# Two-layer gated feed-forward kernel on one core: W_dec in one transfer, gathers in four steps, t's low part on VectorE, new issue orders

## The reference, cut to what matters

```python
# layer 0: a weight matrix of its own for each of 128 sequences, then 8 experts, the best 2 of each token
U = (cond_512 @ W_dec + b_dec).reshape(B, 129, 30)
param = einsum('bik,kj->bij', U, V)
c = einsum('bsd,bde->bse', x, param[:, :-1]) + param[:, -1][:, None]
gate = c @ Wg.T + bg;  w = softmax(top_k(gate, 2))
x = x + sum over the two of w * (W2[e] @ gelu(W1[e] @ c + b1[e]) + b2[e])
# layer 1: layer norms of x with gathered gains and biases, an MLP with a layer norm, then a feed-forward
h = ln(ln(x, pw[id125]), cp[id5]); t = ln(x, tm[id5]); s = ln(x, ms[id3])
m, n, r = x + mlp_ln(memory), x + mlp_ln(noise), x + mlp_ln(resource)
y = ln(silu(concat(w0 h, w1 t, w2 m, w3 n, w4 r, w5 s) @ int_W1 + b1) @ int_W2 + b2, g, be)
f = silu(s1 * (y @ w1)) * (s2 * (y @ w2))
x = x + s5 * (gelu(s4 * (gelu(s3 * (f @ h1)) @ h2)) @ w3)
```

## Time and profile before

| | us |
|---|---|
| median of 3 runs | 443.49 |
| lowest, highest | 441.01, 443.49 |
| the profiled run | 443.04 |
| its span, first to last instruction | 441.2 |
| TensorE busy | 416.0 |
| VectorE busy | 315.6 |
| ScalarE busy | 290.7 |
| GpSimd busy | 142.8 |
| mean granted clock of TensorE | 0.978 |

### The profile page before, as it was taken

The page is one execution under the profiler, slowest core; times in us unless marked ns, Lnnn a source line. Parts: engine busy times, 40 slices in busy tenths (PEclk is TensorE's granted clock), DMA queues, the critical chain, the costliest instruction groups (busy, mean ns, idle before and its releaser), DMA issues.

```text
span 441.2 us, 5719 instructions
## 1 busy us (share of the span) xinstructions
PE 416.0 (94%) x1804; PEld 272.6 (62%) x1804; DVE 315.6 (72%) x651; ACT 290.7 (66%) x515; POOL 142.8 (32%) x129
## 2 busy tenths in 40 slices
...
GB/s 242 364 293 161 179 174 119 112 229 68 104 155 51 71 163 97 118 99 73 111 40 159 75 116 150 0 70 181 134 3 49 46 3 0 1 0 25 0 25 27
DMA packets 29961, 45.08 MB, mean 102 GB/s; under 512 B 3461, under 2 KB 22378, under 8 KB 29418
## 3 DMA queue, kind: packets, MB, share of 16 engines
...
...
## 4 chain that ended last, share of the span: by engine, by line
PE 79%; DVE 8%; ACT 5%; issue 3%; DMA 2%; POOL 2%; another core or an unknown queue 1%; ACTq 0%; POOLq 0%; DVEq 0%
PE bank L644 23%; PE bank L746 20%; PE bank L692 7%; PE bank L636 6%; PE bank L782 6%; PE bank L731 5%; PE bank L823 2%; PE bank L660 2%; DMA muT<-cond_512T_in 2%; PE bank L699 2%; PE bank L771 2%; POOL rstd L1446 1%; ACT mG L890 1%; ACT YN L895 1%
## 5 line engine op out<-in xcount | busy, mean ns | idle before, releaser
L644 PE MATMUL bank<-mG,W 128*128 128x512 f32 x256 | 121.3, 604 | 0.1
L890 ACT ACTIVATE mG<-bank,keepP 128x512 f32<-128x512 f32 x128 | 85.3, 685 | 32.2 <-PE bank L636 30.2
L1446 POOL TENSOR_TENSOR rstd<-ve,mhalf 128x4 f32<-128x4 f32 x24 | 34.0, 1419 | 173.0 <-DVE ve L1196 172.1
L1181 DVE TENSOR_TENSOR mG<-mG,gwbs 128x1024 f32<-128x1024 f32 x64 | 77.1, 1220 | 8.8 <-ACT mG L890 4.4
L644 PEld LDWEIGHTS bank<-mG,W 128*128 128x128 f32 x256 | 48.4, 194 | 44.2 <-issue 39.9
L636 PE MATMUL bank<-ts,A 96*128 96x512 f32 x128 | 66.8, 553 | 1.3 <-ACT mG L890 1.1
L955 ACT ACTIVATE G<-bank,keepP 128x512 f32<-128x512 f32 x48 | 32.8, 696 | 25.4 <-PE bank L746 20.1
L1427 POOL DMA_INDIRECT gp<-pgb_in,ixall x32 | 36.8, 1149 | 27.4 <-DVE norms L1233 17.7
L1430 POOL DMA_INDIRECT gcm<-ctm,ixcm x32 | 36.5, 1140 | 9.8 <-issue 9.8
L746 PE MATMUL bank<-hA_h,h1w_h 128*128 128x512 f32 x96 | 38.9, 405 | 0.0
L746 PE MATMUL bank<-hA_l,h1w_h 128*128 128x512 f32 x96 | 38.6, 402 | 0.0
...
## 6 DMA issues: line engine op xcount, KB each, us to landing
...
```

Of the source, the lines that this page charges most:

```text
L644: mm = pe.matmul(OACC[:, :], W2[:, e * HC + c, :], mG[n % NMG][:, c, :], start=False, stop=(e == E - 1 and c == HC - 1))
L890: act.activation(mG[e % NMG][:, c % HC, :], HM[n % 2][:, :], ACT.Gelu, bias=b1c[:, c:c + 1]).then_inc(m_gelu, 1)
L1181: dve.tensor_tensor(mine, mine, gate.unsqueeze(1).broadcast_to([P, HC, TT, P]), ALU.mult).then_inc(m_q, 1)
L1446: step(pool.tensor_tensor(rstd[:, n, :], ve[:, n, :], mhalf[:, :], ALU.pow))
```

## The change

W_dec comes in one transfer of 128 rows on SP's queue (the halves change their partitions), its last 30 columns (`wd_u`) in one of their own. On ScalarE's queue muT comes first, then `wd_u`, the biases, V, `keepP`, `earlyP`. Piece 7 of the turned W_dec goes to ScalarE. `sq_`, `hs1` and `cs12` move behind G8. The gathers `tab` are issued in four steps of two (`tab0` to `tab3`), each a word of its own in GpSimd's order. `tcl` of blocks 3 to 7 is an instruction of VectorE; blocks 0 to 2 stay on GpSimd. In block 7's feed-forward the copies and low parts of the last two chunks (k of 10 and 11) are single. The order in which the weights are split is h2, h1, w3, w12 instead of h1, h2, w12, w3. All orders are new.

```diff
-        PIECES = ("v", "v", "v", "a", "v", "a", "v", "v")
+        PIECES = ("v", "v", "v", "a", "v", "a", "v", "a")
...
+        def alone(j, k):
+
+            return j is TAIL["p"] and k >= 3 * FC - 2
+
         def tail_lo(eng, j, k):
 
-            eng.wait_ge(p_lo[j.s], j.n * (FC + 4) + (k + 1 if k < FC else FC + (k - FC) // 2 + 1))
+            eng.wait_ge(p_lo[j.s], k + 1 if k < FC else FC + (k - FC) // 2 + 1 + (alone(j, k) and k % 2))
...
             "PE": (
-                (0, "tm0 A0 gm0 A1 sq0 A2 tm1 tm2 gx0 A3 tm3 sq1 tm4 H0 gm1 gm2 H1 H2 tm5 H3 H4 tm6 H5 gm3 sq2 H6 B H7 O0 H8 O1 H9 "
-                    "sq3 H10 H11 O2 H12 H13 O3 H14 gx1 tm7 H15 O4"),
-                (1, "H0 -O5 -O6 H1 H2 -O7 H3 gm4 gm5 H4 -XT H5 H6 B H7 O0 H8 O1 H9 O2 H10 H11 O3 H12 -Tt H13 gm6 H14 H15 gm7 O4"),
...
-                (7, "H0 -O5 H1 =Ts ~F1 H2 -O6 H3 -O7 =Th ~F2 =Z -XT H4 H5 ~F3 B O0 H6 O1 H7 H8 ~F4 H9 ~F5 ~F6 ~F7 =Y O2 H10 -Tt ~F8 "
-                    "-Ts ~F9 -Th ~F10 H11 =YT ~F11 H12 H13 -Z ~F12 =F0 H14 O3 -Y =F1 O4 O5 H15 =F2 O6 O7 =F3 XT -YT -Fr0 =F4 =F5 Tt "
-                    "=F6 Ts =F7 Th -Fr1 Z -Fr2 =F8 Y -Fr3 =F9 =F10 =F11 YT -Fr4 -Fr5 Fp0 -Fr6 -Fr7 =F12 Fp1 -Fr8 Fp2 -Fr9 Fp3 -Fr10 "
-                    "-Fr11 Fp4 Fp5 Fp6 Fp7 -Fr12 Fp8 Fp9 Fp10 Fp11 Fp12"),
+                (0, "tm0 A0 tm1 gm0 sq0 A1 A2 tm2 tm3 gx0 sq1 A3 tm4 tm5 gm1 gm2 H0 H1 H2 H3 H4 sq2 B H5 H6 O0 H7 gm3 H8 O1 H9 H10 "
+                    "O2 H11 H12 sq3 H13 H14 O3 H15 gx1 O4"),
+                (1, "H0 H1 -O5 gm4 H2 -O6 H3 tm6 H4 -O7 H5 tm7 H6 H7 -XT H8 B O0 gm5 H9 O1 H10 H11 O2 H12 O3 H13 O4 H14 H15 gm6 O5"),
...
+                (7, "H0 -O5 H1 ~F1 =Ts H2 -O6 H3 H4 ~F2 =Th -O7 H5 H6 ~F3 =Z -XT B ~F4 H7 ~F5 ~F6 ~F7 H8 H9 -Tt =Y O0 -Ts O1 ~F8 "
+                    "~F9 ~F10 H10 -Th =YT H11 ~F11 H12 -Z ~F12 =F0 -Y O2 =F1 H13 O3 H14 H15 =F2 O4 O5 -YT =F3 O6 O7 XT -Fr0 =F4 =F5 "
+                    "-Fr1 =F6 =F7 Tt -Fr2 Ts =F8 =F9 Th -Fr3 Z =F10 Y =F11 -Fr4 -Fr5 YT -Fr6 -Fr7 Fp0 =F12 Fp1 -Fr8 Fp2 -Fr9 Fp3 "
+                    "-Fr10 -Fr11 Fp4 Fp5 Fp6 Fp7 -Fr12 Fp8 Fp9 Fp10 Fp11 Fp12"),
...
             "ACT": (
-                (0, "gh ah0 aw gel ah1 tch0 gth0 tcg0 ah2 sza gxc0 gxh0 tch1 tcg1 ah3 tch2 tcg2 bh ws g0 g1 tch3 g2 tcg3 g3 smh0 "
-                    "tch4 g4 g5 g6 g7 syc g8 g9 wh1 gth1 g10 g11 wh0 g12 g13 smh1 gxh1 gxc1 g14 g15 tch5 smh2 wh2"),
...
-                    "-nh -tc ~fg8 -sc =ny g9 ~fg9 ~fh8 g10 g11 =ff -ch ~fg10 =fhi ~fg11 ~fh10 g12 -zt =th0 g13 =fh0 =th1 g14 -ny "
-                    "g15 =th2 =fh1 =fh2 =th3 -ff -fhi =fh3 nx -thr0 =fg4 =fg5 =fh4 tc nh sc -fhr0 ch =fg6 -thr1 =fg7 =fh6 -fhr1 zt "
...
+                (0, "aw ah0 gh tch0 tch1 tcg0 tcg1 gel gth0 ah1 bh sza ah2 gxh0 gxc0 tch2 ws ah3 tcg2 wh1 tch3 g0 g1 g2 g3 g4 syc "
+                    "g5 tcg3 g6 wh2 tch4 g7 tcg4 g8 g9 g10 tch5 smh0 wh0 gth1 g11 g12 g13 g14 gxh1 gxc1 g15 smh1"),
...
+                    "=fh1 =th2 -ny g15 =fh2 =th3 -ff -fhi =fh3 -thr0 nx -thr1 =fg4 =fg5 =fh4 =fg6 =fg7 =fh6 tc -fhr0 -thr2 nh sc "
+                    "-fhr1 ch -fhr2 -thr3 zt -fhr3 =fg8 =fg9 =fg10 =fg11 =fh8 ny =fh10 -fgr4 ff fhi -fgr5 -fhr4 thp0 -fgr6 -fgr7 "
...
             "DVE": (
-                (0, "tb0 gl am al0 top0 sv0 gww0 al1 tb1 tb2 gxl0 sv1 al2 sv2 al3 sv3 tb3 sv6 bl tb4 sv4 q0 sml0 q1 top1 q2 q3 gww1 "
-                    "sv5 tb5 q4 q5 wl1 sml1 gxl1 q6 q7 wl2 sml2 wl0 x"),
-                (1, "q0 tb6 -st0 q1 q2 tb7 q3 -t wl3 -hg q4 q5 q6 -s q7 top2 -hc gww2 x -oh gxl2 st0"),
...
-                    "=u0 -st2 q6 =u1 =fl0 oh q7 =u2 =fl1 x =fl2 st0 =u3 -flo =fl3 t hg s -ur0 hc =fl4 -ur1 =fl6 -flr0 a -ur2 st2 "
-                    "-ur3 -flr1 -flr2 -flr3 flo =fl8 =fl10 up0 -flr4 =fo -flr6 up1 flp0 flp1 up2 up3 flp2 flp3 -flr8 -flr10 flp4 "
...
+                (0, "am tb0 sv2 al0 tb1 top0 sv0 gww0 tb2 sv1 gxl0 al1 gl tb3 sv3 sv6 tb4 al2 al3 bl sv4 q0 tcl3 q1 tb5 q2 top1 "
+                    "tcl4 q3 q4 gww1 sv5 q5 wl2 gxl1 tcl5 sml0 sml1 q6 wl1 q7 wl3 wl0 sml2"),
+                (1, "q0 -x q1 -st0 q2 q3 tb6 tb7 q4 q5 tcl6 -hg q6 tcl7 -t q7 top2 -s -oh -hc gww2 x gxl2 st0"),
...
+                (7, "q0 ~fl0 ~u2 q1 ~fl1 ~fl2 ~u3 -x ~fl3 -st0 =a -s -t -hg ~fl4 =st2 ~fl6 -hc q2 -oh ~fl8 ~fl10 =flo q3 -a ~fo q4 "
+                    "=u0 -st2 =u1 oh q5 q6 =fl0 =u2 =fl1 q7 =fl2 =u3 -flo x =fl3 st0 -ur0 s hg -ur1 t =fl4 =fl6 hc -ur2 -ur3 -flr0 "
+                    "a -flr1 -flr2 -flr3 st2 =fl8 =fl10 flo -flr4 up0 =fo -flr6 up1 flp0 up2 flp1 flp2 up3 flp3 -flr8 -flr10 flp4 "
+                    "flp6 -for flp8 flp10 flp11 fop"),
...
             "POOL": (
-                (0, "tcl0 tcl1 tcl2 srt ix tcl3 tab tcl4 tcl5 rt0 tcl6 tcl7 rt1"),
-                (1, "tab rt0 -rt2 rt1"),
...
-                (7, "tab -rt0 -rt1 =rt2 -rt2 rt0 rt1 rt2"),
+                (0, "tcl0 ix tcl1 tcl2 tab0 srt tab1 tab2 tab3 rt0"),
+                (1, "tab0 -rt1 tab1 tab2 rt0 tab3 -rt2 rt1"),
...
+                (7, "tab0 -rt0 -rt1 =rt2 tab1 tab2 -rt2 tab3 rt0 rt1 rt2"),
...
             "SP": (
-                (0, "sgw0 sgp0 sts1 gb0 gb1 sts2 lr sts3 +lt gb2 gb3 sgw1"),
...
+                (0, "sgw0 sgp0 sts1 gb0 lr gb1 +lt sts2 sts3 gb2 gb3 sgw1 sgp1"),
+                (1, "gb0 lr gb1 sts4 vts gb2 sts5 +lt gb3 vtl"),
...
-            load(Wd[0:MU, :], A["W_dec"][:, KR * DH:KR * (D + 1)], ld_wd)
+            load(Wd[:, :], A["W_dec"][:, 0:KR * D].rearrange("m (h c) -> h m c", h=2), ld_wd)
...
-                act.wait_ge(p_g[j.s], j.n * 2 * FC + k - FC + 2)
+                w = 1 if alone(j, k) else 2
+                act.wait_ge(p_g[j.s], k - FC + w)
                 dst = hB if k < 2 * FC else hC
-                act.activation(dst[0][:, c:c + 2, j.cols], j.G[:, c:c + 2, j.cols], ACT.Copy).then_inc(p_hi[j.s], 1)
+                act.activation(dst[0][:, c:c + w, j.cols], j.G[:, c:c + w, j.cols], ACT.Copy).then_inc(p_hi[j.s], 1)
...
-            load(Wd[MU:P, 0:KR * DH], A["W_dec"][:, 0:KR * DH], ld_wd)
             for at in (0, MU):
                 load(muT[at:at + MU, :], A["cond_512T"], ld_wd)
+            load(wd_u, A["W_dec"][:, KR * D:KR * (D + 1)], ld_wd)
+            load(bdec, A["b_dec"][:, 0:KR * D].rearrange("o (i k) -> (o i) k", k=KR), ld_bd)
             load(Vk[:, :], A["V"], ld_v)
             load(keepP[:, :], A["keepP"], ld_v)
-            load(bdec, A["b_dec"][:, 0:KR * D].rearrange("o (i k) -> (o i) k", k=KR), ld_bd)
             load(earlyP[:, :], A["earlyP"], ld_small)
             act.wait_ge(setup0, 1)
             act.activation(warmA[:, 0:64], onesf[:, 0:64], ACT.Copy)
             load(bdec_u, A["b_dec"][:, KR * D:KR * (D + 1)].rearrange("o k -> k o"), ld_bd)
             act.wait_ge(ld_wd, 64)
-            act.wait_ge(wp_zero, 1)
...
+            def tcl(b):
+
+                dve.wait_ge(tc_hi, b + 1)
+                dve.wait_ge(ts_stored[b % 2], 16 * ((b - 1) // 2))
+                dve.wait_ge(tc_lo, b)
+                dve.tensor_tensor(tsS[b % 2][32:64, :], tT[b % 2][:, :], tsS[b % 2][0:32, :].bitcast(F32), ALU.subtract).then_inc(tc_lo, 1)
...
-                    dve.tensor_copy(turned_wd[1][:, mine, :], wd[1][:, mine, :])
-                    dve.tensor_copy(turned_wd[0][:, mine, :], wd[0][:, mine, 0:DH]).then_inc(wd_dve, 1)
-            sq_()
-            step(dve.tensor_scalar(hs1[:, :], fsc[:, 0:FC], 0.5, None, ALU.mult))
-            dve.tensor_tensor(cs12[:, :], hs1[:, :], fsc[:, FC:2 * FC], ALU.mult)
+                    dve.tensor_copy(turned_wd[0][:, mine, :], wd[0][:, mine, :])
+                    dve.tensor_copy(turned_wd[1][:, mine, :], wd[1][:, mine, :]).then_inc(wd_dve, 1)
...
             ins.then_inc(g8_ready, 1)
+            sq_()
+            step(dve.tensor_scalar(hs1[:, :], fsc[:, 0:FC], 0.5, None, ALU.mult))
+            dve.tensor_tensor(cs12[:, :], hs1[:, :], fsc[:, FC:2 * FC], ALU.mult)
...
-            def tables(b):
+            def tables(b, t):
...
-                for t in range(TT):
-                    j = b * TT + t
...
+                j = b * TT + t
...
```

60 lines of the change are left out of this document (30 added, 30 removed), and 77 rows, old and new, of the table ORDER.

## The result

The changed kernel takes 456.38 us (454.54 to 457.3, 4 runs) beside 443.49 for before: ratio 1.0297, 95% interval 1.0248 to 1.0347. It is slower by 3%, where 2.6% faster was predicted. The profiled spans are 454.7 and 441.2 us. I cut both at two points that every run has: the first product `tm0` of block 0, and `XT` of block 7, behind which only block 7's own chain and the feed-forward are left.

What follows compares the result with a forecast made beforehand. TensorE, busy 94% of the span, was taken as the bound, gains lying before 125 and behind 360 us. 441.2 - 3.0 - 4.0 - 3.0 - 1.4 = 429.8 span, 431.6 for the run, 432 us predicted; range 426 to 439.

Steps and rivals of the forecast that it cites:

- Start, -3.0: Setup before tm0: one W_dec transfer and muT first start the copies 3.2 us sooner, at 7.9 us; 3.0 us saved.
- Middle, -4.0: Setup and first blocks: t's low part of blocks 3 to 7 on VectorE saves 4.0 of 5.8 us.
- the wait at L570: Gate products: TensorE's 2.4 us wait in two pieces, behind a slow GpSimd subtraction, would go.
- the 3.4 us of the dip: Clock at 1.2 GHz from 70.4 to 77.2 us, following the gate-product waits; its 3.4 us cost was counted as removed.
- nobody waits for L1181: Sign of being wrong: TensorE waiting for VectorE's L1181 in the first three blocks.
- VectorE becomes the bound: Rival, up to 125 us: VectorE's 90 us of work gives the 5.8 us back; 436 to 439 us, chance 0.22.
- Gathers, 0 within 1: GpSimd's gathers in four steps, with rstd work between pairs: no change in time, bounds -1 and +1 us.
- Orders behind 360, -3.0: Last turn, behind 360 us: new orders remove a 3.2 us wait and its dip, 1.9 us taken back; 3.0 saved.
- Both losses that I priced: Behind 360 us: XT waits for x, +0.8 us, and block 7's Tt waits for t, +0.8 us.
- The 3.2 us wait and its dip: Block 6's feed-forward: Fr0's wait for its input's low part goes, with the clock dip behind it: -3.2 and -1.7 us.
- Last chunks, -1.4: Very end, after the last GELU: single copies and subtractions instead of pairs save 1.4 us; called the surest term.
- The one that ended slower: Rival: O products wait over 2 us in each block and the clock dips anew; 450 us, chance 0.07.

Runs made afterwards that it cites:

- x2: Changed kernel with W_dec laid out in DRAM as 128 rows ahead of the launch, still one transfer: 435.86 us, ratio 0.9819 to before.
- x1: Changed kernel with W_dec in two transfers of 64 rows, both on SP's queue, one behind the other: 436.27 us, ratio 0.9821 to before.
- z3: x1 with turn 0 reordered: A3 ahead of sq1, ah3 ahead of ws, al1 to al3 earlier: 434.99 us, ratio 0.981 to before.
- z4: x1 with a block's four gather steps together and the roots ahead of or behind all eight gathers: 443.21 us, ratio 0.9992 to before.
- z2: Kernel before with W_dec's second half moved to SP's queue, the 30 last columns staying in the first half's rows: 440.98 us, ratio 0.9956.
- y2: Kernel before with single last chunks and the changed kernel's last-turn order on TensorE, ScalarE and VectorE: 439.1 us, ratio 0.9903.
- y1: Kernel before with only the last two chunks' copies and low parts made single: 441.73 us, ratio 0.9953.

## Why the prediction was wrong, step by step

- **Start, -3.0: the step that failed.** "Nothing shows one transfer of both halves; I bound it from both sides", 7.0 to 8.5 us. Both bounds took for granted that the transfer runs at the rate of the halves of the earlier trace rows, on all engines. The diff showed a leading dimension of 2; it landed at 28.9. That is the whole loss: +19.3 us instead of -3.0. The lower bound of 7.0 didn't hold for a well laid transfer either: x2's rows were there at 5.2 us. Without the slow view the start gives 1.4 (x1), 2.0 (z3) or 3.0 us (z4) by their profiles, and 2.7 in z2's form. "wd_u ... I cost it at nothing, hidden behind the weight" was wrong too: in x1 its rows ended last, 1.0 us behind the weight's (8.42 and 7.39), and the copies began 1.3 us later than in z2. And the last bias transfer, of which I wrote "It moves ahead too", moved by only 0.9 us in x1 (additions from 15.68), not by 3.2. That the clock would dip there again was right, at 1.2 GHz from 11.7 to 35.6 us after, but with only 4.68 us of TensorE's work in it.
- **Middle, -4.0: right pieces, wrong whole.** It gained 1.4 us (0.3 by the points of the table). The subtractions take 0.681 us against 0.69 predicted, the wait at L570 is gone, nobody waits for L1181, and from 144 us TensorE has no idle time. But the 3.4 us of the dip were counted as owned by that wait. Removing the wait took 2.4 us away; other waits came in with the new orders (between 30 and 40 us in x1, 51 and 60 in the changed kernel), and a dip of the clock followed them, 10.2 us long, 13.7 in x1. Idle time fell by 1.3 us (2.1 without `XT`'s wait, which belongs to the end) and half of the low clock rose by 1.7. How much of the dip the orders made stays open, as its length differs between kernels with the same orders. "VectorE becomes the bound" is not what happened: what TensorE waited for did come from VectorE, but it was setup values (`gwT_l`, A's low part) and their place in the order, not q.
- **Gathers, 0 within 1: wrong for these orders.** In the new orders the steps are worth about 7 us.
- **Orders behind 360, -3.0: right, by its own path.** y2 less y1 is 2.6 us of time, and 4.4 at the end less the 1.1 that moved ahead of the dividing point. Both losses that I priced came, 0.79 for `XT` and 1.21 for `Tt` against 0.8 and 0.8, together 2.0 of the 1.9 us taken back. The 3.2 us wait and its dip went as said.
- **Last chunks, -1.4:** 1.3 by the end of y1.
- **The rivals.** None held what happened. The one that ended slower looked for waits in each block, and none put a price on a transfer that is late by itself, though in the earlier trace rows the copies, and so the whole setup, start with the last landing.
